# Column maxima of the slot logits: spread to all partitions by two DMAs through memory in place of TensorE products and VectorE copies

## The chip, the cores and the metric

The kernel runs on one core of a Trainium2 chip. The metric is the device time of one launch in microseconds (us), as the median of several executions; lower is better. Five engines work side by side and meet only at semaphores: TensorE (PE; PEld is its weight load), VectorE (DVE), ScalarE (ACT), GpSimd (POOL) and SyncE (SP), which issues all DMAs of this kernel.

## The reference, cut to what matters

A cross-attention block is followed by a soft mixture of experts. The change lies in the second part. With two batches of 1024 tokens, 16 experts of 64 slots (1024 slots in all) and width 256:

```python
logits   = einsum('bnd,esd->bnes', x, se)                 # tokens by slots
dispatch = softmax(logits, axis=1)                        # over the tokens: one maximum a slot
combine  = softmax(logits.reshape(b, n, -1), axis=-1)     # over the slots: one maximum a token
slots    = einsum('bnd,bnes->besd', x, dispatch)
# 16 experts: gelu(slots @ Wg + bg) * (slots @ Wu + bu), then @ Wd + bd
out      = einsum('bns,bso->bno', combine, eout)
```

The softmax over tokens needs, for each batch and slot, the maximum over all 1024 tokens. The tokens lie in the 128 partitions (rows) and in 8 tiles of 128, the slots along the free axis, so the maximum has to be taken across partitions, and its negative has to be present in every partition before it can be added to the logits.

## The kernel before, in words

The program is a list of events, one list for all engines (`prologue + attention + logits + slots + experts + combine`). Each engine walks through the list in its own `step` function and does its part of each event. TensorE takes the list as it stands; VectorE, ScalarE and GpSimd take it through `later(...)`, which sorts the events by their place in the list plus an offset from a table (`LATER_SLOTS_ACT`, `LATER_SLOTS_DVE`, `LATER_SLOTS_POOL`). The place is an index, so an event that is taken out of one place and put in at another can change which of two other events comes first on an engine.

The events around the change, with the lines of the profile:

- `("x2T", i)`: TensorE transposes the normalized tokens of tile i (L1534); ScalarE and VectorE write them as a high and a low half, GpSimd makes another low half (L757). Before it, `("N2", i)` normalizes tile i on VectorE (L1213) and then, in two operations, on GpSimd (L752, L753).
- `("L", i)`: the logits of token tile i, 12 TensorE products of 512 columns (L1552); ScalarE copies them into `lsb` (L922), VectorE takes them into the running maximum `colmax` (L1235), SP stores them to memory (L625). There are 16 tiles, 8 a batch. `("A", i)`: VectorE's maximum of each token (L1240).
- `("MX", b, c)`: for batch b and half c of the slots (512 of them), TensorE transposes `colmax` in four pieces (L1561), and VectorE reduces them to `nb`, 128 partitions by 4, the negated maxima, one slot a partition (L1248).
- `("MB", b, c)`: TensorE multiplies `nb`, broadcast along the free axis, with the identity, four products of 128 by 128 (L1570), which leaves the 512 values in every partition; VectorE copies them to `nb_b` (L1253). As `nb` has room for one batch, the reduction for batch 1 waits for the product of batch 0.
- `("E", n)`: n counts 16 blocks of 128 slots, 8 a batch. GpSimd adds `nb_b` to the logits of the block (L773), into one of three buffers `disp_f`; ScalarE takes the exponential (L932). It is the only reader of `nb_b`. Blocks 0 to 3 read half 0 of batch 0, 4 to 7 half 1, 8 to 11 and 12 to 15 those of batch 1.
- `("H", n)`: ScalarE copies the high half of block n (L943), VectorE makes the low half (L1260). `("D", n)`: 24 TensorE products (L1585) of dispatch weights and tokens; the first 16 need the high half alone, the last 8 the low half. VectorE divides by the sum (L1266, L1267). `("sT", n)`: the transpose of the result (L1593).

Events that leave a result in one of the three accumulator banks (`acc_no`) take the banks in turn, and TensorE waits for the bank's reader three events back. SP is a queue in order: 16 stores of logits tiles, then a wait for eight blocks of `E` (L627), the bias loads (L633) and the loads of the expert weights (L645).

The batches' events stand like this before: `MX(0,0)` after `L(8)`, `MB(0,0)` after `L(10)`, `MX(0,1)` after `L(11)`, `MB(0,1)` after `L(13)`; after `L(15)` come `H(0) D(0) MX(1,0) H(1) MX(1,1) MB(1,0)`, and `MB(1,1)` follows `D(1)`.

Of the kernel before, what the change touches and what calls it, by code (L numbers as in the profile page):

```python
# [5 lines left out]
P = 128  # L6
# [84 lines left out]
    ("HT", 14), ("EO", 13), ("CT", 0, 0), ("HT", 15), ("CT", 0, 1), ("EO", 14), ("EO", 15), ("COa", 0),  # L91
]
SLOTS_HEAD = [
    ("H", 0), ("D", 0), ("MX", 1, 0), ("H", 1), ("MX", 1, 1), ("MB", 1, 0),
]
LOGITS_AT = {3: [('B', 0)], 8: [('MX', 0, 0)], 10: [('MB', 0, 0)], 11: [('E', 0), ('MX', 0, 1)], 12: [('E', 1)], 13: [('MB', 0, 1)], 15: [('E', 2)]}
LATER_SLOTS_ACT = {
# [78 lines left out]
def program(nc, io):  # L176
# [94 lines left out]
    for ev in prologue + attention + logits + slots + experts + combine:  # L271
        if ev[0] == "Y" and ev[1] == GROUPS - 1:
            continue
        if ev[0] in ("bias", "cT", "K", "V", "VT", "xT", "Q", "PV", "Y", "seT", "x2T", "MX", "MB", "D", "sT", "HT", "EO", "CO"):
            acc_no[ev] = len(acc_no)
        if ev[0] == "T":
            t_no[ev] = len(t_no)
        if ev[0] == "S":
            s_no[ev] = len(s_no)
        if ev[0] == "V":  # L280
            v_no[ev] = len(v_no)
        if ev[0] in ("cT", "K", "VT", "xT", "Q", "PV", "seT", "x2T", "sT", "HT"):
            high_no[ev] = len(high_no)
# [9 lines left out]
    in_order(later(logits + slots, LATER_SLOTS_ACT), {("W", e, w): no for (e, w), no in piece_no.items()})  # L293
    in_order(later(logits + slots, LATER_SLOTS_DVE), acc_no)
    in_order(later(experts, LATER_EXPERTS_DVE) + combine, acc_no)

    top = ExitStack()
    top.enter_context(nc.allow_non_contiguous_dma(reason="three bias vectors, one value a partition"))

    def sb(stack, name, shape, dt=F32):  # L300
        return stack.enter_context(nc.sbuf_tensor(name, shape, dt))
# [92 lines left out]
    colmax = sb(lg, "colmax", [P, B, ES])  # L394
    nb_b = sb(lg, "nb_b", [P, B, ES])
    den = sb(lg, "den", [P, 2])
    nb = sb(lg, "nb", [P, ST])
    slot_f = sb(lg, "slot_f", [P, 2, D])
    b_row_at = -(-nc.sbuf_base // 32) * 32
    lg.close()  # L400
# [90 lines left out]
    last_full, last_used = sem("last_full"), sem("last_used")  # L491
    l_full, l_ready, amax_ready, colmax_ready = sem("l_full"), sem("l_ready"), sem("amax_ready"), sem("colmax_ready")
    d_shift, d_exp, d_high, d_low = (sem(s) for s in ("d_shift", "d_exp", "d_high", "d_low"))
    b_pick_ready, b_zeros = sem("b_pick_ready"), sem("b_zeros")
    w_high, gate_low, up_low, down_low, down_low_dve, b_high, b_low, eo_high = (sem(s) for s in (
        "w_high", "gate_low", "up_low", "down_low", "down_low_dve", "b_high", "b_low", "eo_high"))
# [72 lines left out]
    def _(sp):  # L569
# [49 lines left out]
        sp.dma_start(sb_b[:], slot_b.unsqueeze(0).to_broadcast([P, D])).then_inc(d_se, 16)  # L619
        sp.dma_start(sc_b[:], scale.unsqueeze(0).to_broadcast([P, 1])).then_inc(d_se, 16)  # L620
        l_t = logits_dram.rearrange("(t p) s -> p t s", p=P)
        for i in range(TILES):

            sp.wait_ge(l_ready, 2 * (i + 1))
            sp.dma_start(l_t[:, i], lsb[:, i]).then_inc(d_lst, 16)  # L625

        sp.wait_ge(d_shift, ST)  # L627
        sp.wait_ge(colmax_ready, TB)
# [35 lines left out]
    def _(pool):  # L664
# [15 lines left out]
        def step(ev):  # L680
# [48 lines left out]
            elif ev[0] == "Y" and ev[2] == 1:  # L729
                g = ev[1]  # L730

                pool.wait_ge(mv2_ready, 2 * g + 2)
                v = mv2[:, 2 * g:2 * g + 2, 1]
                link(pool.tensor_tensor(norm2[:, 0], v, eps[:], ALU.add))
                link(pool.tensor_tensor(norm2[:, 1], norm2[:, 0], mhalf[:, 0:2], ALU.pow))
                link(pool.tensor_tensor(norm2[:, 2], v, norm2[:, 1], ALU.mult))
                link(pool.tensor_tensor(norm2[:, 3], norm2[:, 2], norm2[:, 1], ALU.mult))
                link(pool.tensor_tensor(norm2[:, 4], norm2[:, 3], eps[:], ALU.add))
                link(pool.tensor_tensor(norm2[:, 5], norm2[:, 4], mhalf[:, 0:2], ALU.pow))
                pool.tensor_tensor(rstd2[:, 2 * g:2 * g + 2], norm2[:, 5], norm2[:, 1], ALU.mult)\  # L740
                    .then_inc(rstd2_ready, 1)
            elif ev == ("SA", ST // 2):
                pool.wait_ge(se_var, 1)
                link(pool.tensor_tensor(srs[:, 0], smv[:, :, 1], eps[:, 0:1].to_broadcast([P, ST]), ALU.add))
                pool.tensor_tensor(srs[:, 1], srs[:, 0], mhalf[:], ALU.pow).then_inc(se_rstd, 1)
            elif ev[0] == "N2":
                i = ev[1]

                pool.wait_ge(x2_centered, i + 1)
                if i == 0:  # L750
                    pool.wait_ge(d_gain, 32)
                link(pool.tensor_tensor(x2f[:, i % 3], x2f[:, i % 3], gain[:], ALU.mult))  # L752
                pool.tensor_tensor(x2f[:, i % 3], x2f[:, i % 3], shift[:], ALU.add).then_inc(x2_ready, 1)  # L753
            elif ev[0] == "x2T":
                i = ev[1]
                pool.wait_ge(x2_high, i + 1)
                pool.tensor_tensor(x2[1][:, i, 0:D], x2f[:, i % 3], x2[0][:, i, 0:D], ALU.subtract).then_inc(x2_low, 1)  # L757
            elif ev[0] == "E":
                n = ev[1]
                b, t = divmod(n, ST)  # L760

                wait_used(pool, ("MB", b, 2 * t // ST))
                if n < 3:

                    if n == 2:
                        wait_done(pool, ("MX", 0, 1))
                    wait_used(pool, ("seT", ST - 1))
                else:

                    pool.wait_ge(d_exp, n - 2)  # L770
                    if n == 3:
                        pool.wait_ge(d_low, 1)
                pool.tensor_tensor(disp_f[n % 3][:], lsb[:, b * TB:(b + 1) * TB, t * P:(t + 1) * P],  # L773
                                   nb_b[:, b, t * P:(t + 1) * P].unsqueeze(1).to_broadcast([P, TB, P]), ALU.add)\
                    .then_inc(d_shift, 1)
            elif ev[0] == "W" and ev[1:] not in FIRST_LOW_DVE:
                weight_low(ev[1], ev[2])
            elif ev == ("B", 0):

                pool.wait_ge(last_used, 2)  # L780
                pool.memset(b_row[:].bitcast(F32), 0.0).then_inc(b_zeros, 1)
# [235 lines left out]
    def _(dve):  # L1017
# [34 lines left out]
        def step(ev):  # L1052
# [188 lines left out]
            elif ev[0] == "MX":  # L1241
                _, b, c = ev

                wait_done(dve, ev)
                if b:

                    wait_done(dve, ("MB", 0, c))
                dve.tensor_reduce(nb[:, 4 * c:4 * c + 4], acc(no).rearrange("p (t n) -> p t n", t=4), AX, ALU.max,  # L1248
                                  negate=True).then_inc(acc_free, 1)
            elif ev[0] == "MB":  # L1250
                _, b, c = ev
                wait_done(dve, ev)
                dve.tensor_copy(nb_b[:, b, c * 512:(c + 1) * 512], acc(no)).then_inc(acc_free, 1)  # L1253
            elif ev[0] == "H":
                n = ev[1]
                dve.wait_ge(d_high, n + 1)
# [84 lines left out]
    def _(pe):  # L1341
# [31 lines left out]
        def step(ev):  # L1373
# [182 lines left out]
            elif ev[0] == "MX":  # L1556
# [4 lines left out]
                    ins = pe.transpose(dst[:, t * P:(t + 1) * P], colmax[:, b, (4 * c + t) * P:(4 * c + t + 1) * P],  # L1561
                                       ident[:])
                ins.then_inc(acc_full, 1)
            elif ev[0] == "MB":
                _, b, c = ev
                dst = bank(ev)

                wait_used(pe, ("MX", b, c))
                for t in range(4):
                    ins = pe.matmul(dst[:, t * P:(t + 1) * P], nb[:, 4 * c + t:4 * c + t + 1].to_broadcast([P, P]),  # L1570
                                    ident[:], start=True, stop=True)
                ins.then_inc(acc_full, 1)
            elif ev[0] == "D":
                n = ev[1]
                b = n // ST
# [116 lines left out]
```

## Time and profile before

| | us |
|---|---|
| median of 3 executions | 544.42 |
| lowest, highest | 544.23, 544.68 |
| the profiled execution | 544.24 |
| span in its profile (first to last instruction) | 542.5 |
| PE, DVE, ACT, POOL busy | 530.0, 434.1, 402.2, 303.3 |

The profiled execution is the lowest but for 0.01 us; 1.7 us of it lie outside the span. Engine times in the profile are counted from the start of the span. A row of a timeline gives start, length, engine, line, operation, the tiles written and read, and how many instructions were merged; in brackets, the idle time before it and what ended it. Two operations that follow each other on an engine overlap by nearly 0.1 us, so what an operation takes out of its engine's time is the distance of two starts.

### The profile page before, as it was taken

The numbers are of one execution on the slowest core, as the hardware profiler recorded it, in microseconds if no ns is written. First come the engines' busy times: TensorE is split into PE (matmuls) and PEld (weight loads), VectorE is DVE, ScalarE is ACT, GpSimd is POOL, SyncE is SP. The second block draws the span as 40 slices with busy tenths as digits, with TensorE's granted clock in tenths as the row PEclk, the third lists the DMA queues.
The fourth block names the chain that finished last, engine by engine and source line by source line (L and its number), as shares of the span: only waits on it lengthen the run. The fifth ranks groups of instructions, "written<-read, shape, count | busy, mean of one in ns | idle before, by whom it ended". The sixth has DMA issues, their size and how long they took to land.

```text
span 542.5 us, 11967 instructions
## 1 busy us (share of the span) xinstructions
PE 530.0 (98%) x3896; PEld 499.8 (92%) x3896; DVE 434.1 (80%) x1305; ACT 402.2 (74%) x1098; POOL 303.3 (56%) x327
## 2 busy tenths in 40 slices
PE   6999999999999999999998999999999999999997
PEld 4889999999999999999997888999978888899997
DVE  6777878787897979899677998798699888865453
ACT  5879969596896959779564555788979889766562
POOL 6674654544545455454365768787467999910000
DMA  8635000000030000000001333150288888525551
GB/s 257 181 86 179 3 1 2 2 2 1 3 98 2 2 2 1 2 0 4 0 1 80 155 156 156 78 201 1 79 264 283 270 306 288 182 79 170 181 167 67
DMA packets 34901, 54.11 MB, mean 100 GB/s; under 512 B 3997, under 2 KB 21497, under 8 KB 34713
## 3 DMA queue, kind: packets, MB, share of 16 engines
q1 hardware_dynamic: 34841, 53.36, 29.7%
q8 instruction: 32, 0.52, 0.4%
q14 instruction: 28, 0.23, 0.1%
HBM read 40.54 MB, written 10.49 MB: 94 GB/s over the span
## 4 chain that ended last, share of the span: by engine, by line
PE 90%; ACT 4%; DMA 2%; POOL 1%; DVE 1%; issue 1%; SPq 0%; ACTq 0%; DVEq 0%
PE ps L1461 9%; PE ps L1585 9%; PE ps L1357 9%; PE ps L1369 8%; PE ps L1610 8%; PE ps L1499 8%; PE ps L1439 7%; PE ps L1552 7%; PE ps L1476 5%; PE ps L1632 4%; PE ps L1501 4%; PE ps L1644 3%; DMA wvo_raw<-in_L_xattn_Wo_dram 2%; ACT expo L885 1%; PE ps L1615 1%; PE ps L1622 1%
## 5 line engine op out<-in xcount | busy, mean ns | idle before, releaser
L885 ACT ACTIVATE expo<-expo,nmin 128x154 f32<-128x154 f32 x256 | 106.2, 423 | 5.3 <-DVE nmin L1135 4.8
L1135 DVE CUSTOM_DVE_ANT_0 expo<-ps,maskb 128x154 f32<-128x154 f32 x256 | 69.1, 312 | 11.9 <-PE ps L1461 11.9
L723 POOL TENSOR_TENSOR prob_t<-expo,prec 128x104 f32<-128x104 f32 x64 | 23.1, 360 | 89.3 <-DVE prec L1146 89.1
L726 POOL TENSOR_TENSOR prob<-expo,prec 128x512 f32<-128x512 f32 x64 | 66.8, 1043 | 0.0
L1461 PE MATMUL ps<-kbd,qT_high 128*128 128x308 f32 x256 | 61.1, 323 | 0.0
L1155 DVE TENSOR_TENSOR pT_low<-ps,pT_high 128x512 fp32r<-128x512 f32 (+1 forms) x96 | 57.2, 596 | 4.1 <-ACT pT_high L899 3.9
L788 POOL TENSOR_TENSOR w_gu_low<-w_raw,w_gu_high 128x1024 fp32r<-128x1024 f32 x17 | 50.3, 2966 | 16.2 <-ACT w_gu_high L835 16.1
L899 ACT CAST pT_high<-ps 128x512 fp32r<-128x512 f32 (+1 forms) x96 | 49.1, 513 | 10.8 <-PE ps L1476 8.1
L803 ACT ACTIVATE oT_high<-ps,bqv_c 128x256 fp32r<-128x256 f32 x64 | 29.8, 466 | 34.8 <-PE ps L1501 34.7
L885 ACT ACTIVATION_READ_ACCUMULATOR expo<-expo,nmin 128x1 f32 x256 | 50.3, 196 | 0.0
L1461 PEld LDWEIGHTS ps<-kbd,qT_high 128*128 128x128 f32 x256 | 39.8, 190 | 0.2
L1461 PE MATMUL ps<-kbd,qT_low 128*128 128x308 f32 x128 | 39.0, 304 | 0.0
L1476 PE MATMUL ps<-ident,prob 128*128 128x128 f32 x256 | 38.5, 273 | 0.1
L1369 PE MATMUL ps<-wvo_high,oT_high 128*128 128x256 f32 x128 | 37.0, 289 | 0.0
L1501 PE MATMUL ps<-pT_high,vt 104*128 104x256 f32 x128 | 36.3, 284 | 0.0
L1369 PE MATMUL ps<-wvo_high,oT_low 128*128 128x256 f32 x128 | 36.2, 283 | 0.0
L1369 PE MATMUL ps<-wvo_low,oT_high 128*128 128x256 f32 x128 | 36.0, 281 | 0.0
L1357 PE MATMUL ps<-eo_high,comb 128*128 128x256 f32 x256 | 34.6, 287 | 0.4 <-issue 0.4
L1032 DVE SCALAR_TENSOR_TENSOR oT_low<-ps,bqv_c,oT_high 128x256 fp32r<-128x256 f32 x64 | 30.3, 474 | 5.3 <-ACT oT_high L803 4.5
L922 ACT COPY lsb<-ps 128x512 f32<-128x512 f32 x32 | 17.2, 589 | 22.3 <-PE ps L1552 22.3
L1006 ACT CAST comb<-ps 128x512 fp32r<-128x512 f32 x32 | 17.2, 590 | 21.3 <-PE ps L1644 21.3
L1032 DVE SCALAR_TENSOR_TENSOR qT_low<-ps,bqv_c,qT_high 128x256 fp32r<-128x256 f32 x64 | 29.9, 468 | 3.7 <-ACT qT_high L803 3.6
(241 smaller groups left out, 1762.7 us busy)
## 6 DMA issues: line engine op xcount, KB each, us to landing
logits_dram<-lsb SPq DMA_DIRECT2D x16, 512.0 KB, 2.6
w_raw<-in_L_ffn_Wg_dram SPq DMA_DIRECT2D x16, 512.0 KB, 4.0
w_raw<-in_L_ffn_Wu_dram SPq DMA_DIRECT2D x16, 512.0 KB, 4.5
w_raw<-in_L_ffn_Wd_dram SPq DMA_DIRECT2D x16, 512.0 KB, 4.5
lraw<-logits_dram SPq DMA_DIRECT2D x13, 512.0 KB, 3.8
out_dram<-gate SPq DMA_DIRECT2D x16, 128.0 KB, 2.2
kbd<-keys SPq DMA_DIRECT2D x12, 154.0 KB, 2.8
wvo_raw<-in_L_xattn_Wv_dram SPq DMA_DIRECT2D x2, 512.0 KB, 7.0
```

Of the source, the lines that this page charges most:

```text
L726: pool.tensor_tensor(prob[:, n % 2, :, heads, :], expo[:, n % 2, pp, :, :, 0:P], prec[:, n % 2, pp].unsqueeze(3).to_broadcast([P, 2, 2, P] ...
L788: pool.tensor_tensor(low, w_raw[:, i % RAW].rearrange("p (k n) -> p k n", k=KD if w == 0 else FT), high, ALU.subtract).then_inc(low_made(e ...
L885: ins = act.activation(row, row, ACT.Exp, scale=-1.0, bias=nmin[:, n % 2, pp, j, h:h + 1], accum_out=psums[:, n % 2, pp, j, h:h + 1])
L899: act.copy(pT[0][0:rows, n % 2, 2 * t:2 * t + tiles], ps[0:rows, NS + k % NT, 0:tiles * 2 * P].rearrange("p (t n) -> p t n", t=tiles))\
L1032: dve.scalar_tensor_tensor(out=dst, in0=src, scalar=bias, in1=high, op0=ALU.add, op1=ALU.subtract)\
L1135: ins = dve.tensor_tensor_reduce(out=expo[:, n % 2, pp, j, h, :], in0=ps[:, s % NS, h * SK:(h + 1) * SK], in1=maskb[:, (2 * (n // QUADS) + ...
L1155: dve.tensor_tensor(pT[1][0:rows, n % 2, 2 * t:2 * t + tiles], ps[0:rows, NS + k % NT, 0:tiles * 2 * P].rearrange("p (t n) -> p t n", t=ti ...
L1357: ins = pe.matmul(dst[:, 0:D], combT[s][:, i % 2, t], eo[m][:, i // TB, t], start=(first and r == 0 and t == parts[0]), stop=(last and r = ...
L1369: ins = pe.matmul(dst, oT[s][:, p, j * P:(j + 1) * P], wo[m][:, p], start=(first and p == 0 and r == 0), stop=(last and p == PAIRS - 1 and ...
L1461: ins = pe.matmul(dst, qT[s][:, n % 2, pp, j * P:(j + 1) * P], kbd[:, b, m, p, :], start=(r == 0), stop=(r == 2))
L1476: ins = pe.transpose(ps[:, NS + k % NT, (2 * h + j) * P:(2 * h + j + 1) * P], prob[:, n % 2, j, 2 * t + h, 0:P], ident[:])
L1501: ins = pe.matmul(dst[:, 0:2 * P], vt[:, b, s, q, pp * P:(pp + 1) * P], pT[m][0:T4, n % 2, 4], start=False, stop=(r == 2))
```

## The change

`MB` is no event of TensorE and VectorE any more. SP does it, in the place that `MB` has in the list: it waits until `nb` is written, stores the 128 by 4 values to a row of 512 floats in memory, waits for that store, and loads the row into all 128 partitions of `nb_b`. GpSimd's `E` waits for the load. `nb` gets room for both batches, so the reduction for batch 1 waits for nothing but its own transposes. `MB` takes no accumulator bank any more. In the list, each `MB` now stands right behind its `MX` (but `MB(1,1)`, which stays behind `D(1)`), and the logits stores keep their order around it on SP.

```diff
 SLOTS_HEAD = [
-    ("H", 0), ("D", 0), ("MX", 1, 0), ("H", 1), ("MX", 1, 1), ("MB", 1, 0),
+    ("H", 0), ("D", 0), ("MX", 1, 0), ("MB", 1, 0), ("H", 1), ("MX", 1, 1),
 ]
-LOGITS_AT = {3: [('B', 0)], 8: [('MX', 0, 0)], 10: [('MB', 0, 0)], 11: [('E', 0), ('MX', 0, 1)], 12: [('E', 1)], 13: [('MB', 0, 1)], 15: [('E', 2)]}
+LOGITS_AT = {3: [('B', 0)], 8: [('MX', 0, 0), ('MB', 0, 0)], 11: [('E', 0), ('MX', 0, 1), ('MB', 0, 1)], 12: [('E', 1)], 15: [('E', 2)]}
...
-        if ev[0] in (..., "x2T", "MX", "MB", "D", "sT", "HT", "EO", "CO"):
+        if ev[0] in (..., "x2T", "MX", "D", "sT", "HT", "EO", "CO"):
             acc_no[ev] = len(acc_no)
...
+    nb_order = [ev[1:] for ev in logits + slots if ev[0] == "MX"]
+    nb_dram = nc.dram_tensor("column_max", (B, ES), F32, kind="Internal").ap()
...
-    nb = sb(lg, "nb", [P, ST])
+    nb = sb(lg, "nb", [P, B, ST])
...
-        for i in range(TILES):
-
-            sp.wait_ge(l_ready, 2 * (i + 1))
-            sp.dma_start(l_t[:, i], lsb[:, i]).then_inc(d_lst, 16)
+        def spread_max(b, c):
+
+            k = nb_order.index((b, c)) + 1
+            row = nb_dram[b, c * 512:(c + 1) * 512]
+            wait_used(sp, ("MX", b, c))
+            sp.dma_start(row.rearrange("(t p) -> p t", p=P), nb[:, b, 4 * c:4 * c + 4]).then_inc(d_nb_row, 16)
+            sp.wait_ge(d_nb_row, 16 * k)
+            sp.dma_start(nb_b[:, b, c * 512:(c + 1) * 512], row.unsqueeze(0).to_broadcast([P, 512])).then_inc(d_nb[b][c], 16)
+
+        for ev in logits + slots:
+            if ev[0] == "L":
+                i = ev[1]
+                sp.wait_ge(l_ready, 2 * (i + 1))
+                sp.dma_start(l_t[:, i], lsb[:, i]).then_inc(d_lst, 16)
+            elif ev[0] == "MB":
+                spread_max(ev[1], ev[2])
...
-                wait_used(pool, ("MB", b, 2 * t // ST))
+                pool.wait_ge(d_nb[b][2 * t // ST], 16)
...
                 wait_done(dve, ev)
-                if b:
-
-                    wait_done(dve, ("MB", 0, c))
-                dve.tensor_reduce(nb[:, 4 * c:4 * c + 4], ...
+                dve.tensor_reduce(nb[:, b, 4 * c:4 * c + 4], ...
-            elif ev[0] == "MB":
-                _, b, c = ev
-                wait_done(dve, ev)
-                dve.tensor_copy(nb_b[:, b, c * 512:(c + 1) * 512], acc(no)).then_inc(acc_free, 1)
...
-            elif ev[0] == "MB":
-                _, b, c = ev
-                dst = bank(ev)
-
-                wait_used(pe, ("MX", b, c))
-                for t in range(4):
-                    ins = pe.matmul(dst[:, t * P:(t + 1) * P], nb[:, 4 * c + t:4 * c + t + 1].to_broadcast([P, P]),
-                                    ident[:], start=True, stop=True)
-                ins.then_inc(acc_full, 1)
```

With the places of `MB` in the list, two neighbours change on other engines: on VectorE `A(8)` comes before `N2(12)` (it came behind it), and on ScalarE the order `H(0) E(1) L(15) H(1) E(2) H(2)` becomes `H(0) L(15) E(1) E(2) H(1) H(2)`. On TensorE and GpSimd the order of the events that remain is the same.

## Rows read from the trace of the kernel before

**Rows 1.** Waits of PE, 288 to 395 us: total, times, longest.
```profile
PE ps L1534 <- POOL x2f L753: 1.1, 1, 1.1
...
PE ps L1570 <- DVE nb L1248: 0.6, 1, 0.6
```
**Rows 2.** Waits of PE, 395 us to the end.
```profile
PE ps L1357 <- issue: 0.4, 1, 0.4
```
**Rows 3.** Chain that ended last, 320 to 352 us: start, us, what.
```profile
333.85 0.89 PE ps L1570 x8
...
340.53 2.89 PE ps L1585 x24
343.42 0.45 PE ps L1561 x4
...
348.93 0.89 PE ps L1570 x8
```
**Rows 4.** Timeline of PE, 318 to 357 us.
```profile
324.25 0.38 PE L1534 MATMUL ps<-ident,x2f 128*128 128x128 f32 x2
...
334.58 0.38 PE L1534 MATMUL ps<-ident,x2f 128*128 128x128 f32 x2
...
340.37 1.12 PE L1585 MATMUL ps<-x_high,disp_high 128*128 128x258 f32 x8
...
345.77 1.21 PE L1585 MATMUL ps<-x_high,wkq_high 128*128 128x258 f32 x8
```
**Rows 5.** Timeline of VectorE, 318 to 357 us.
```profile
319.41 0.68 DVE L1248 TENSOR_REDUCE nb<-ps 128x4 f32<-128x512 f32 x1
...
320.66 1.21 DVE L1240 TENSOR_REDUCE neg_amax<-lsb 128x1 f32<-128x1024 f32 x1
321.79 1.27 DVE L1235 TENSOR_TENSOR colmax<-ps,colmax 128x512 f32<-128x512 f32 x2
...
325.96 0.67 DVE L1253 COPY nb_b<-ps 128x512 f32<-128x512 f32 x1
326.56 0.41 DVE L1030 TENSOR_TENSOR x2T_low<-ps,x2T_high 128x256 fp32r<-128x256 f32 x1
...
341.78 1.28 DVE L1235 TENSOR_TENSOR colmax<-ps,colmax 128x512 f32<-128x512 f32 x2
```
**Rows 6.** Timeline of GpSimd, 318 to 357 us.
```profile
321.63 0.74 POOL L753 TENSOR_TENSOR x2f<-x2f,shift 128x256 f32<-128x256 f32 x1
...
328.86 2.41 POOL L773 TENSOR_TENSOR disp_f<-lsb,nb_b 128x1024 f32<-128x1024 f32 x1
...
332.10 0.74 POOL L752 TENSOR_TENSOR x2f<-x2f,gain 128x256 f32<-128x256 f32 x1 [0.23 <-DVE x2f L1213]
332.92 0.74 POOL L753 TENSOR_TENSOR x2f<-x2f,shift 128x256 f32<-128x256 f32 x1
...
355.30 2.40 POOL L773 TENSOR_TENSOR colmax<-lsb,nb_b 128x1024 f32<-128x1024 f32 x1 [0.86 <-ACT ps L932]
```
**Rows 7.** Timeline of ScalarE, 318 to 357 us.
```profile
341.76 1.03 ACT L943 CAST wkq_high<-ps 128x1024 fp32r<-128x1024 f32 x1
343.16 1.03 ACT L932 ACTIVATE ps<-colmax 128x1024 f32<-128x1024 f32 x1 [0.36 <-DVE colmax L1235]
```
**Rows 8.** DMA issues: count, KB each, median us from issue to landing.
```profile
logits_dram<-lsb SPq DMA_DIRECT2D x16, 512.0 KB, 2.6
...
bo_b<-in_L_xattn_bo_dram SPq DMA_DIRECT2D x1, 128.0 KB, 7.3
...
b_raw<-in_L_ffn_bu_dram SPq DMA_DIRECT2D x1, 32.0 KB, 1.8
...
sc_b<-in_L_ffn_scale_dram SPq DMA_DIRECT2D x1, 0.5 KB, 5.1
```
**Rows 9.** The tile `keys`, SP's time for an issue: ns min/median/max.
```profile
L607 SPq DMA_DIRECT2D kbd<-keys x12: 590/610/1367, 17.9 to 31.0; - x12
```
**Rows 10.** Waits of SP over the span: total, times, longest.
```profile
SPq L633 <- POOL disp_f L773: 9.3, 1, 9.3
```

More of the change, by code:

```diff
@@ L273, in program @@
             continue
-        if ev[0] in ("bias", "cT", "K", "V", "VT", "xT", "Q", "PV", "Y", "seT", "x2T", "MX", "MB", "D", "sT", "HT", "EO", "CO"):
+        if ev[0] in ("bias", "cT", "K", "V", "VT", "xT", "Q", "PV", "Y", "seT", "x2T", "MX", "D", "sT", "HT", "EO", "CO"):
             acc_no[ev] = len(acc_no)
@@ L295, in program @@
     in_order(later(experts, LATER_EXPERTS_DVE) + combine, acc_no)
+    nb_order = [ev[1:] for ev in logits + slots if ev[0] == "MX"]
+    assert [ev[1:] for ev in logits + slots if ev[0] == "MB"] == nb_order
+    nb_dram = nc.dram_tensor("column_max", (B, ES), F32, kind="Internal").ap()
     top = ExitStack()
@@ L493, in program @@
     d_shift, d_exp, d_high, d_low = (sem(s) for s in ("d_shift", "d_exp", "d_high", "d_low"))
+    d_nb_row, d_nb = sem("d_nb_row"), [[sem(f"d_nb{b}{c}") for c in range(2)] for b in range(B)]
     b_pick_ready, b_zeros = sem("b_pick_ready"), sem("b_zeros")
@@ L1244, in step @@
                 wait_done(dve, ev)
-                if b:
-                    wait_done(dve, ("MB", 0, c))
-                dve.tensor_reduce(nb[:, 4 * c:4 * c + 4], acc(no).rearrange("p (t n) -> p t n", t=4), AX, ALU.max,
+                dve.tensor_reduce(nb[:, b, 4 * c:4 * c + 4], acc(no).rearrange("p (t n) -> p t n", t=4), AX, ALU.max,
                                   negate=True).then_inc(acc_free, 1)
-            elif ev[0] == "MB":
-                _, b, c = ev
-                wait_done(dve, ev)
-                dve.tensor_copy(nb_b[:, b, c * 512:(c + 1) * 512], acc(no)).then_inc(acc_free, 1)
             elif ev[0] == "H":
```

## The prediction

> **What bounds the kernel now.** I read the views in this order: the waits of TensorE, the chain that ended last around the change, the timelines of the four engines there, and the DMA issues. The waits of TensorE say that it sets the pace: from 288 to 395 us, where logits and dispatch lie, it waits 1.1 us at the start (a normalization on GpSimd), 0.6 in front of one `MB` for `nb` [rows 1], and else only at the very end of the stage; from 395 us on it waits 0.4 us in all [rows 2]. None of the `D` products waits for its operands. So a microsecond that leaves TensorE's queue here is won at the end, if no other engine takes up the slack. The chain runs through the `MB` products, 0.89 us each [rows 3]. The timelines must then tell how far behind TensorE the others are, and there the margin is thin.
>
> **What is removed, and what then holds TensorE.** Four `MB` of four products leave TensorE, at 0.89 us each [rows 3], and four copies leave VectorE, each taking 326.56 - 325.96 = 0.60 us of it [rows 5]. I go along the list.
>
> (1) `MB(0,0)`. Without it TensorE would come to the transpose `x2T(12)` at 324.25 - 0.89 = 323.36 us [rows 4]. But on VectorE `A(8)` now stands ahead of `N2(12)`. `A(8)` takes 321.79 - 320.66 = 1.13 us [rows 5], so `N2(12)` is that much later, and GpSimd's second half of it ends at 321.63 + 0.74 + 1.13 = 323.50 [rows 6]; with some 0.14 us for the semaphore TensorE starts at 323.64. That gives 324.25 - 323.64 = 0.61, not 0.89.
>
> (2) `MB(0,1)`. TensorE's next transpose, `x2T(15)`, started at 334.58 [rows 4] and could come 0.61 + 0.89 = 1.50 earlier, at 333.08. It needs `N2(15)`, for which GpSimd had waited 0.23 us on VectorE [rows 6]; VectorE is ahead by its one copy so far, 0.60. GpSimd's end moves from 332.92 + 0.74 = 333.66 to 333.06, and with 0.14 the transpose starts at 333.20. Gain so far: 334.58 - 333.20 = 1.38. The last two logits tiles follow without a gap, and `D(0)` starts 1.38 earlier.
>
> (3) From `D(0)` to `D(1)`. Before, 345.77 - 340.37 = 5.40 us [rows 4]. Two `MX` of 0.45 behind the 2.89 of `D(0)` [rows 3] would leave 3.79. But ScalarE now does `E(2)` ahead of `H(1)`. `E(2)` needs the maximum of tile 15: VectorE's two operations for it end at 341.78 + 1.28 = 343.06, 2.69 behind the start of `D(0)`, and nothing in front of them is faster now (the low half of block 0, which waits for the end of `L(15)`). So `E(2)` starts 2.79 behind `D(0)`, as before, at 343.16 against 340.37 [rows 4, 7]; `H(1)`, which used to run ahead of it at 341.76, starts some 0.95 later, takes 1.03 [rows 7], and with 0.12 for the semaphore `D(1)` starts 2.79 + 0.95 + 1.03 + 0.12 = 4.89 behind `D(0)`. Gain 5.40 - 4.89 = 0.51; without the new order it would be 1.6. What is late next is the low half of block 1; at the 1.21 us of VectorE's other operation on 128 by 1024 [rows 5] it is done before `D(1)` asks for it, 16 of its 24 products or 1.9 us later.
>
> (4) `MB(1,1)` between `D(1)` and `sT(0)`: 0.89 [rows 3]. VectorE is two copies lighter there, so the other blocks keep their margin. `H(1)` lies later against TensorE than before, and `E(3)` with it, but 16 products of `D(1)` and all of `D(2)` lie ahead of the use.
>
> Sum: 1.38 + 0.51 + 0.89 = 2.78 us. Two smaller edits cost nothing: `nb` for two batches takes a wait away that had long been met, and with fewer takers of banks the tightest is `D(1)` on the bank of `D(0)`, whose two short readers on VectorE run while TensorE does the `MX` and waits for `H(1)`.
>
> **What is added.** Four pairs of DMAs, in series, on SP. The trace before shows neither, so I bound a pair from both sides. The store has 512 pieces of 4 bytes. SP took 0.61 us to issue 256 pieces (64 partitions by 4 runs) [rows 9], so 1.2 us for 512; the smallest loads landed 1.8 us after issue [rows 8], which holds about 0.4 of issue. That gives 1.8 + 0.8 = 2.6 us. The load has 128 pieces of 2 KB, 256 KB: between 1.8 us for 32 KB and 2.6 for 512 KB [rows 8], I take 2.4. A pair is then about 5.2 us with its two semaphores. The lower bound is 3.6 (twice 1.8). The upper is 12.4: the one load of 4-byte pieces landed after 5.1 us and the first row spread to all partitions after 7.3 [rows 8], both behind other transfers. I take 5.2, nearer the low end, because SP's queue holds only one logits store a tile here, which lands in 2.6.
>
> The Trainium skill, "DMA: Bandwidth & Descriptors", section "Rules for kernel authors", speaks against the store: a last dimension that is not contiguous becomes a descriptor for each element, and should be rearranged. By its section "Anatomy of one DMA", with about 2.0 us fixed for each transfer (given for another issuing path) and the bytes at 436 GB/s, a pair would be an estimated 4.6 us, and the sum above would stay as it is. The 1.8 us of the smallest loads agrees with the first figure; no row shows the price of 512 elements.
>
> What hides the pairs: `nb(0,0)` is written at 319.41 + 0.68 = 320.09 [rows 5], and `E(0)` began at 328.86, straight behind other work of GpSimd [rows 6]; it would begin at 328.26. A pair may take 8.2 us, 8.4 with the 0.2 us that GpSimd waits later. The other three have more: `MX(0,1)` lies a stage earlier than its first reader `E(4)`, and `nb(1,0)`, reduced behind transposes that end at 343.42 + 0.45 = 343.87 before [rows 3], is read by `E(8)` at 355.30 [rows 6], 11 us behind; both come earlier after. Behind SP's waits stand logits stores, which nobody awaits until the bias loads, and there SP had idled 9.3 us for GpSimd [rows 10]; two pairs end within that, as the second one's store need not wait for the first one's load. If the cover is gone, `E(0)` holds up `N2(15)` behind it on GpSimd, that `x2T(15)`, and each microsecond beyond 8.4 is one lost.
>
> The profiled execution took 544.24: 544.24 - 2.78 = 541.46. The median of the runs is 0.18 higher, so I forecast 541.6.
>
> **Rivals.** *The full price of the products.* If neither `N2(12)` nor `H(1)` comes late, all four `MB` and the wait in front of the third are won: 0.89 + 0.89 + (5.40 - 3.79) + 0.89 = 4.28, 540.1 on the median's scale. For it: the waits show only what happened before. Against: both orders are in the code, and the rows give them lengths. Chance 0.08.
>
> *The gain goes back in the dispatch stage.* If some `D(n)` now waits for its low half, what is won from `D(1)` on (0.51 + 0.89) is lost and 1.38 stays: 543.0. For it: VectorE and ScalarE are busy there as well, and `H(1)` starts behind TensorE's clock by a microsecond more. Against: no `D` waited in 50 us [rows 1] and VectorE has two copies less. Chance 0.10.
>
> *The first pair is slow.* The place is `E(0)` on GpSimd. At 8.4 us nothing is lost, at 8.4 + 2.78 = 11.2 us all is given back, and at the upper bound of 12.4 the kernel takes 541.6 + 4.0 = 545.6, slower. For it: 512 pieces of 4 bytes, and the 7.3 and 5.1 us of the nearest forms. Against: those stood in a queue of large loads. Chance 0.10, with about half of it beyond 11.2.
>
> **How the numbers follow.** The forecast, 541.6 give or take 0.5, has 0.72. The range for 8 in 10 runs from 540.4 to 543.1; it leaves out the full price below and most of the slow pair above. A difference of 0.2%, 1.1 us, is about what a measurement of this kernel can tell from no change. Faster by more than that: the forecast, the full price, most of the second rival and a little of the third, 0.87. The same: 0.07. Slower: a pair beyond 12.3 us or something that I don't see, 0.06.
>
> **What would show it.** In the profile after, no L1570 and no L1253 row; `x2T(12)` waits 0.3 us on GpSimd and `x2T(15)` 0.1; `D(1)` starts 4.9 us behind `D(0)`, with about 1.1 us of waiting for ScalarE's `H(1)`; no `E` waits for a DMA; the `D` stage keeps its period; the experts run as before, 2.8 us earlier. It is wrong if GpSimd's first `E` waits for `nb_b`, if `D(2)` to `D(15)` show waits, or if `H(1)` runs in time.

## The result, and the profile after

The kernel after takes 556.18 us (median of 4 executions, 554.66 to 557.87), the kernel before beside it 544.55 (544.23 to 545.21): ratio 1.0214, 95% interval 1.0193 to 1.0236. The prediction was 541.6, in a range from 540.4 to 543.1. The change makes the kernel slower by 11.6 us.

The profiled execution took 557.58 us, 13.34 more than the profiled one of before, and its span is 555.6; TensorE's mean granted clock was 0.988. The four executions lie at 554.7, 554.8, 557.6 and 557.9 us, with mean granted clocks of 0.991, 0.993, 0.988 and 0.988, so the profiled one is of the slower two, and what follows accounts for its 13.3 us, not for the 11.6 of the medians.

Waits of TensorE from 288 to 420 us, beside [rows 1]; total, times, longest:

```profile
PE ps L1545 <- POOL x2f L771: 6.2, 2, 5.1
PE ps L1587 <- ACT disp_high L961: 5.4, 1, 5.4
```

L1545 are the `x2T` transposes, L1587 the `D` products. Of the 6.2, 1.1 is the wait at the start of the stage that [rows 1] has too. Two waits of over 5 us are new. The chain that ended last names what released them (start, us, what):

```profile
320.09 8.98 DMA column_max<-nb
...
329.08 4.72 DMA nb_b<-column_max
...
338.43 0.66 PE ps L1545 x2
...
374.74 4.83 DMA b_raw<-in_L_ffn_bd_dram
...
379.59 0.03 ACT b_row L979
...
382.21 5.50 PE ps L1587 x24
```

The first pair of DMAs and the last bias load have entered the chain, where the prediction had all of them hidden. The first pair takes from 320.09 to 333.8, 13.7 us, where 5.2 were predicted and 8.4 were covered: 8.98 for a store of 2 KB, then 4.72 for the load. On GpSimd, `E(0)` and `E(8)` wait over 5 us for a load (and `E(12)` 3.37); beside [rows 6]:

```profile
333.86 2.34 POOL L791 TENSOR_TENSOR disp_f<-lsb,nb_b 128x1024 f32<-128x1024 f32 x1 [5.57 <-DMA nb_b<-column_max]
...
366.06 2.40 POOL L791 TENSOR_TENSOR colmax<-lsb,nb_b 128x1024 f32<-128x1024 f32 x1 [5.77 <-DMA nb_b<-column_max]
```

The other three pairs are no faster. SP's timeline (L633 store, L635 load, L651 bias loads; logits stores are left out; the length is that of the issue alone):

```profile
320.09 0.37 SPq L633 DMA_DIRECT2D column_max<-nb  x1
329.08 0.32 SPq L635 DMA_DIRECT2D nb_b<-column_max  x1
...
331.23 0.98 SPq L633 DMA_DIRECT2D column_max<-nb  x1
344.50 0.32 SPq L635 DMA_DIRECT2D nb_b<-column_max  x1
...
351.13 0.37 SPq L633 DMA_DIRECT2D column_max<-nb  x1
361.22 0.32 SPq L635 DMA_DIRECT2D nb_b<-column_max  x1
361.58 0.43 SPq L633 DMA_DIRECT2D column_max<-nb  x1
373.39 0.32 SPq L635 DMA_DIRECT2D nb_b<-column_max  x1
373.90 0.34 SPq L651 DMA_DIRECT2D b_raw<-in_L_ffn_bg_dram  x1
```

Each load's issue follows the landing of its store: 9.0, 13.3, 10.1 and 11.8 us behind the store's. SP is an ordered queue, so each late store pushes what stands behind it: logits stores, the next pair, and at the end the bias loads, which go out at 373.90. The waits of SP answer to [rows 10]: the 9.3 us in which SP waited for GpSimd in front of the bias loads are gone, and it waits 41.9 for its own stores:

```profile
SPq L635 <- DMA column_max<-nb: 41.9, 4, 12.3
```

The data of the first store are through long before it counts as landed. Stretches of the trace: length, each engine's busy time (instructions), granted clock, busy share of the 16 DMA engines, GB/s:

```profile
321.00:322.00 1.00, 1.00 (x7) 0.83 (x6) 1.00 (x3) 1.00 (x3) 0.09 (x1) 1.00 0.25 2
322.00:324.00 2.00, 2.00 (x12) 1.60 (x11) 2.00 (x5) 0.65 (x4) 1.92 (x3) 1.00 0.00 0
...
355.00:361.00 6.00, 6.00 (x53) 6.00 (x51) 5.96 (x11) 4.38 (x8) 5.23 (x3) 1.00 0.00 0
367.00:373.00 6.00, 6.00 (x53) 6.00 (x52) 4.33 (x11) 3.87 (x7) 6.00 (x3) 1.00 0.00 0
```

From 322 us the DMA engines move nothing, and the store counts as landed at 329.08: seven microseconds in which the trace shows nothing but its completion outstanding. The same stands behind each of the four stores: the DMA engines are idle from about 322.0, 337.3, 354.1 and 366.0 us, and the stores count as landed 7.1 to 7.4 us later. In what comes before that, 1.9 to 6.1 us, the four differ, and there, besides the store's own data, logits stores or the load of the pair before are moving.

The Trainium skill, "DMA: Bandwidth & Descriptors", section "Anatomy of one DMA", says that a transfer's semaphore fires only when its last byte is confirmed in the target memory, and that HBM is the heaviest target for this; it puts the whole fixed cost at about 2 us (for another issuing path). The order of events agrees with this trace, the size does not.

The rest of the loss is TensorE's clock. The same view, around the two gaps of TensorE:

```profile
333.00:337.00 4.00, 0.36 (x2) 0.00 (x0) 0.00 (x0) 0.76 (x1) 3.14 (x3) 1.00 1.00 392
337.37:344.19 6.82, 5.76 (x16) 4.63 (x17) 3.17 (x5) 2.22 (x7) 6.74 (x6) 0.53 0.00 0
...
381.74:388.57 6.83, 6.36 (x31) 6.39 (x32) 5.55 (x10) 5.96 (x12) 4.53 (x2) 0.53 0.62 206
389.00:407.00 18.00, 17.88 (x150) 17.64 (x148) 12.17 (x30) 16.64 (x29) 8.51 (x4) 1.00 0.21 61
```

In each of the two gaps of TensorE, which had been busy up to them, the granted clock fell from 2.4 GHz to its lower level, 1.2 GHz (0.53 of full speed in each of the two stretches shown), and it stayed there for some 6.8 us, into the work behind the gap. Timeline of TensorE, with the idle time in brackets, beside [rows 4]:

```profile
338.43 0.66 PE L1545 MATMUL ps<-ident,x2f 128*128 128x128 f32 x2 [5.07 <-POOL x2f L771]
346.70 1.13 PE L1587 MATMUL ps<-x_high,disp_high 128*128 128x258 f32 x8
...
351.61 1.22 PE L1587 MATMUL ps<-x_high,wkq_high 128*128 128x258 f32 x8 [0.95 <-ACT wkq_high L961]
...
382.21 2.06 PE L1587 MATMUL ps<-x_high,disp_high 128*128 128x258 f32 x8 [5.41 <-ACT disp_high L961]
```

With the same starts in the trace of before, the distances on TensorE give the account, us:

| stretch | before | after | difference |
|---|---|---|---|
| start to `x2T(11)` | 320.32 | 320.75 | +0.43 |
| `x2T(11)` to `x2T(15)` | 14.26 | 17.68 | +3.42 (5.07 of waiting, less 1.8 for two `MB`) |
| `x2T(15)` to `D(0)`, two logits tiles | 5.79 | 8.27 | +2.48 (lower clock) |
| `D(0)` to `D(2)` | 9.42 | 8.03 | -1.39 (the gain of `MB(1,0)`, `MB(1,1)`) |
| `D(2)` to `D(8)` | 18.74 | 18.72 | 0 |
| `D(8)` to `D(9)` | 3.10 | 8.76 | +5.66 (bias loads, below) |
| `D(9)` to `D(11)` | 6.22 | 8.86 | +2.64 (lower clock) |
| `D(11)` to `D(15)` | 12.42 | 12.43 | 0 |

The sum is 13.2 of the 13.34. `D(9)` waits for the high half of its block, `H(9)` on ScalarE; in front of `H(9)` stands the conversion of the expert biases to `b_row` (L979), and that waits 7.36 us for the last bias load, which SP could issue only behind the fourth pair:

```profile
379.59 1.26 ACT L979 CAST b_row<-b_raw 16x1280 fp32r<-16x1280 f32 x1 [7.36 <-DMA b_raw<-in_L_ffn_bd_dram]
```

### The profile page after: what moved, and what is told of

Its sections match the earlier page's. It is cut to its first block, busy times and chain, and to the rows that moved or that the text cites. A ratio compares the mean times of both kernels' runs of the same rounds, so it can differ in the third digit from the quotient of the medians.

```text
span 555.6 us, 11901 instructions
## 1 busy us (share of the span) xinstructions
PE 532.0 (96%) x3864; PEld 500.2 (90%) x3864; DVE 432.0 (78%) x1301; ACT 402.4 (72%) x1098; POOL 303.3 (55%) x327
## 2 busy tenths in 40 slices
DMA packets 37589, 55.17 MB, mean 99 GB/s; under 512 B 6173, under 2 KB 23673, under 8 KB 37401
## 4 chain that ended last, share of the span: by engine, by line
PE 80%; DMA 6%; DVE 5%; ACT 4%; issue 2%; POOL 2%; SPq 0%; DVEq 0%; ACTq 0%
PE ps L1472 8%; PE ps L1368 8%; PE ps L1380 8%; PE ps L1612 8%; PE ps L1587 8%; PE ps L1510 8%; PE ps L1450 7%; PE ps L1487 4%; PE ps L1634 4%; PE ps L1512 4%; PE ps L1646 3%; PE ps L1563 2%; DMA wvo_raw<-in_L_xattn_Wo_dram 2%; DMA column_max<-nb 2%; ACT expo L903 1%
## 5 line engine op out<-in xcount | busy, mean ns | idle before, releaser
L791 POOL TENSOR_TENSOR disp_f<-lsb,nb_b 128x1024 f32<-128x1024 f32 x11 | 26.2, 2387 | 15.9 <-DMA nb_b<-column_max 8.9
L1061 DVE TENSOR_TENSOR w_gu_low<-w_raw,w_gu_high 128x1024 fp32r<-128x1024 f32 x14 | 30.4, 2171 | 3.6 <-ACT w_gu_high L853 3.6
```

## The experiments

Every kernel below starts from the kernel after. Their own ratios are to runs of the kernel before on the same chip.

### Without the pairs

```diff
-            elif ev[0] == "MB":
-                spread_max(ev[1], ev[2])
+                if i == 3:                    # behind logits store 3
+                    for b, c in ...:
+                        sp.dma_start(nb_b[...], const_dram[b]...to_broadcast([P, 512]))
```

> This kernel leaves the column maxima out: nb_b gets a constant a batch (-220 and -56), loaded from memory at the fourth logits tile, and no store or load of maxima is issued; all else is as in the changed kernel, with the new orders on VectorE and ScalarE. Theory 1 (all of the loss comes from the pairs of DMAs being late, and the sum of the prediction is right without them): 541.6 us, 2.8 below the kernel before, no wait of GpSimd for a DMA, D(1) about 4.9 us behind D(0). Theory 2 (the new orders, or the bank count, cost time by themselves): at or above 544. Theory 3 (the products were worth their full price): 540.1.

Measured: 542.54 us (541.72 to 543.48), ratio 0.9961, 0.9946 to 0.9976; profiled execution 541.72. Of TensorE's waits in the logits and dispatch stages the longest, beside the one at the start, is the predicted one in front of `D(1)`:

```profile
PE ps L1598 <- ACT wkq_high L970: 1.0, 1, 1.0
```

The time is 2.2 us below that of the kernel before by the medians (1.3 to 2.9 by the interval) and 2.5 by the profiled executions, where the prediction had 2.78. So what the edits on TensorE, VectorE and ScalarE do together agrees with the prediction within the noise, and the loss lies in the pairs.

### What the delay reaches: the biases, `E(0)`, and both

`bias_ahead` issues the bias loads between the last store and its load:

```diff
             sp.dma_start(row.rearrange("(t p) -> p t", p=P), nb[...]).then_inc(d_nb_row, 16)
+            if (b, c) == (1, 1):
+                load_biases()
             sp.wait_ge(d_nb_row, 16 * k)
```

> The changed kernel, but SP issues the three bias loads between the store and the load of the last pair, so that they wait for no pair but the third. Theory 1 (the loss has two places, E(0) behind the first pair and the bias copy on ScalarE behind SP's waits; each brings a stretch of TensorE at the lower clock): the 5.4 us wait of D(9) for H(9) and its slow stretch of some 3 us go, the wait of 5.1 us in front of x2T(15) stays; about 548, 547 to 550. Theory 2 (D(9) is held by the late load of the last pair through E(12), not by the biases): 554 or more, and the wait of D(9) stays.

`e0_later` gives GpSimd's `E(0)` a place behind `N2(15)` and the low half of `x2T(14)`, so that it holds up no transpose, and leaves the bias loads where they were:

```diff
 LATER_SLOTS_ACT = {
-    "GU": 3.5, ("E", 0): 6, ...
+    "GU": 3.5, ("E", 0): 12, ...
 LATER_SLOTS_POOL = {
-    ... ("MX", 1, 1): -0.5, ("E", 0): -0.5, ...
+    ... ("MX", 1, 1): -0.5, ("E", 0): 8, ("E", 1): 3, ...
```

> The changed kernel, but E(0) stands behind N2(15) and the low half of x2T(14) on GpSimd, E(1) behind the low half of x2T(15), and E(0) behind L(14) on ScalarE. Theory 1: the 5.1 us wait in front of x2T(15) and the slow clock after it (some 2.5 us) go, the wait of D(9) stays: about 549, 548 to 551. Theory 2 (the pairs slow TensorE by their traffic, or the logits stores held back on SP are what is missed): no gain, 555 or more.

`both` has the two edits together.

> The edits of bias_ahead and e0_later together; the stores and loads of the maxima are as slow as in the changed kernel. Theory 1: both losses go and the gain of the removed products is left, 542 to 543.5. If part of the loss has a third place (a late E(4) or E(12), traffic): above 545.

Measured: `bias_ahead` 550.83 us (549.38 to 554.57), ratio 1.0123, 1.0085 to 1.0161. `e0_later` 555.97 (554.67 to 557.22), 1.0215, 1.0192 to 1.0238: no gain at all. `both` 551.06 (549.53 to 551.77), 1.0113, 1.0093 to 1.0133: no better than `bias_ahead` alone. In `bias_ahead` the wait of `D(9)` is gone and the one in front of `x2T(15)` stays, as its theory 1 said; the median lies 0.8 above that theory's range:

```profile
PE ps L1550 <- POOL x2f L776: 4.6, 1, 4.6
```

The slow stretch behind this gap is shorter than in the kernel after: the granted clock is 0.50 from 338 to 340 us and 1.00 again from 342, and the two logits tiles up to `D(0)` take 7.27 us, not 8.27. So what a gap costs on top of itself was not one figure.

The waits of TensorE in `e0_later`, from 310 to 420 us:

```profile
PE ps L1587 <- DVE sT_low L1285: 4.8, 1, 4.8
PE ps L1587 <- ACT disp_high L961: 2.7, 1, 2.7
```

The 5.07 us in front of `x2T(15)` is gone, as intended, and `D(0)` starts at 338.80. But SP has not become faster. Its timeline in `e0_later`, third and fourth pair:

```profile
347.02 0.55 SPq L633 DMA_DIRECT2D column_max<-nb  x1
362.47 0.32 SPq L635 DMA_DIRECT2D nb_b<-column_max  x1
362.83 0.43 SPq L633 DMA_DIRECT2D column_max<-nb  x1
372.12 0.32 SPq L635 DMA_DIRECT2D nb_b<-column_max  x1
372.63 0.34 SPq L651 DMA_DIRECT2D b_raw<-in_L_ffn_bg_dram  x1
```

The third store, issued 4.1 us earlier than in the kernel after, lands 1.2 us later. What `E(0)` no longer costs is waited for at `D(8)`, since `E(8)` needs the third load, and at `D(9)`, since the biases go out at 372.63. The releaser that the row names in front of `D(8)`, `sT_low`, is the end of that chain: ScalarE waits 6.34 us for `E(8)`, and only behind `E(8)`, `H(8)` and `E(9)` does it copy the `sT` whose accumulator bank `D(8)` takes. So `e0_later` has the time of its theory 2, but by neither of the causes that the theory gave. In `both` the biases are out of the way. GpSimd waits there for the second and the fourth load too (4.2 us at `E(4)`, 2.3 at `E(12)`), but only its wait for the third, at `E(8)`, reaches TensorE. Waits of GpSimd and of TensorE in `both`:

```profile
POOL colmax L796 <- DMA nb_b<-column_max: 7.1, 1, 7.1
POOL disp_f L796 <- DMA nb_b<-column_max: 6.5, 2, 4.2
...
PE ps L1592 <- DVE sT_low L1290: 4.5, 1, 4.5
```

There are thus three places at which the series of stores holds TensorE, `E(0)`, `E(8)` and the biases, one behind the other. My account of the kernel after had two, since there TensorE, late already by `E(0)`, has no wait at `D(8)`. Mending the places, with the stores as slow as they are, brought the kernel to 550.8 us at best, still above the kernel before.

### Why the store is slow: shape against number

`store_16B` writes the same bytes to the row in another order: 128 pieces of 16 bytes, each partition's four values side by side.

```diff
-            sp.dma_start(row.rearrange("(t p) -> p t", p=P), nb[...])
+            sp.dma_start(row.rearrange("(p t) -> p t", t=4), nb[...])
```

The row then holds the slots in another order.

> The changed kernel with one edit: the store writes the 4 values of a partition side by side, so it has 128 pieces of 16 bytes and not 512 of 4. The row in memory is then in another order than the slots, so each slot gets the maximum of another slot of its half as its shift. Theory 1 (the time of the store goes with its pieces: about 7.3 of its 9 us lie behind the moment when its data have passed the DMA engines, and 512 pieces are four times 128): the first store lands after 3.5 to 4.2 us; the first pair takes 8.5 us and E(0) waits at most 1; the biases are in time; the kernel takes 542 to 543.5. Theory 2 (a store to memory takes 9 us here whatever its pieces, because of the logits stores around it): 9 us again, 554 to 558.

`store_apart` keeps the 512 pieces of 4 bytes, but writes them 512 bytes apart. The loads bring a constant row.

```diff
-    nb_dram = nc.dram_tensor("column_max", (B, ES), F32, kind="Internal").ap()
+    nb_dram = nc.dram_tensor("column_max", (B, ES, P), F32, kind="Internal").ap()
-            row = nb_dram[b, c * 512:(c + 1) * 512]
+            row = nb_dram[b, c * 512:(c + 1) * 512, 0]
```

> The store keeps its 512 pieces of 4 bytes but writes them 512 bytes apart from each other in memory; the load takes a row of constants (-220 and -56 by batch, written at 150 us) in place of the maxima, still behind the store. This leaves the maxima out. Theory 1 (the price goes by the piece): the store lands after 9 us alone, 9 to 15 behind logits stores, as in the changed kernel, 555 to 558 in all. Theory 2 (the price comes from pieces of different partitions that fall into the same stretch of memory): 2.5 to 4 us, 542 to 544. For the load: 4.7 us again if that is what a row for all partitions costs; 2.4 to 3 if it was slow because the row had just been written.

`spacing` looks for the distance at which the effect ends:

```diff
+            n = (4, 8, 16, 32)[2 * b + c]       # 16, 32, 64, 128 bytes
+            row = nb_dram[2 * b + c, 0:512 * n].rearrange("(s n) -> s n", n=n)[:, 0]
```

> Where 4-byte pieces stop to disturb each other. The four stores write 512 pieces of 4 bytes each, 16, 32, 64 and 128 bytes apart in this order; the loads bring a constant row, so the maxima are left out. Theory 1 (a store is slow while pieces of several partitions fall into one short stretch of memory, and the stretch is 64 bytes or so): the store at 16 bytes 5 to 9 us, at 32 bytes 3 to 6, at 64 and 128 bytes 1.8 to 2.5 as with 512 bytes. Theory 2 (the stretch is 512 bytes): all four are slow, 128 bytes 3 us or more. Theory 3 (it is enough that the pieces are not next to each other): all four land in 1.8 to 2.5. Time 542 to 548, by whether the first, second and third store land late.

Measured: `store_16B` 541.94 us (540.89 to 543.81, 10 executions), ratio 0.9959, 0.9945 to 0.9972. `store_apart` 542.42, one execution. `spacing` 544.74, one execution, so of these two the rows count and not the times; what it has more than `store_apart` it has ahead of the first pair (`x2T(11)` at 322.82 against 320.11). SP's timeline in `store_apart`, first pair, and in `spacing`, the stores at 16, 32 and 128 bytes with the issue of the load behind them:

```profile
319.88 0.37 SPq L639 DMA_DIRECT2D column_max<-nb  x1
321.71 0.32 SPq L642 DMA_DIRECT2D nb_b<-constant_row  x1
```

```profile
322.16 0.37 SPq L640 DMA_DIRECT2D column_max<-nb  x1
324.59 0.32 SPq L643 DMA_DIRECT2D nb_b<-constant_row  x1
...
331.69 0.37 SPq L640 DMA_DIRECT2D column_max<-nb  x1
333.66 0.32 SPq L643 DMA_DIRECT2D nb_b<-constant_row  x1
...
348.25 0.42 SPq L640 DMA_DIRECT2D column_max<-nb  x1
351.55 0.32 SPq L643 DMA_DIRECT2D nb_b<-constant_row  x1
```

512 pieces of 4 bytes land 1.8 us after issue when they are 512 bytes apart, and 2.4, 2.0, 2.0 and 3.3 at 16, 32, 64 and 128 bytes; the last goes out right behind a load of 256 KB, as that of `store_apart`, which takes 3.1. Side by side they take 9.0 to 13.3 (15.4 in `e0_later`). So it is not the number of pieces, which the count of DMA packets under 512 bytes confirms: 6173 in the kernel after and 6461 in `store_apart`, which has two rows of constants more, against 4637 where the four stores have 128 pieces each (`strided`, below). It is that pieces of 4 bytes, which come from neighbouring partitions, lie side by side. Theory 3 of `spacing` holds, but for the store behind the load, and the other two fall. 16 bytes written as one piece next to 16 bytes of the next partition are fast too: 2.2 and 1.9 us for the first two stores of `store_16B`, less than the 3.5 to 4.2 that its theory 1 worked out from a quarter of the pieces. Neither a distance of 8 bytes nor separate pieces of one partition side by side were tried, and what it is in the memory that delays the completion stays open.

For the load, `store_apart` gives 3.2 us in the median for a row of constants written long before, and the versions that read a row just written give 3.6 to 3.7. So having just been written is worth at most half a microsecond of the 4.7 in the kernel after; there three logits stores go out right behind the first load, and no run separates what they add.

The Trainium skill, "DMA: Bandwidth & Descriptors", section "Rules for kernel authors", advises against a last dimension that is not contiguous, as it becomes a descriptor for each element. The advice is right here, but for another reason than the one it gives: `store_apart` has a descriptor for each element as well, and is fast.

### The row made by TensorE

```diff
+    pe.transpose(dst[0:4, 0:P], nb[:, b, 4 * c:4 * c + 4], ident[:])     # event MB, behind MX
+    dve.tensor_copy(nb_t[:, b, c], acc(no)[0:4, 0:P])
-    sp.dma_start(row.rearrange("(t p) -> p t", p=P), nb[...])
+    sp.dma_start(row.rearrange("(t p) -> t p", p=P), nb_t[:, b, c])      # 4 pieces of 512 bytes
```

> TensorE transposes the 128 by 4 maxima (one product of 128 columns) and VectorE copies the 4 by 128 result, so that the store has 4 pieces of 512 bytes; the load is as in the changed kernel. MB stands behind L(9) for the first half, behind L(13) and D(1) for the others, and ScalarE keeps the order of the kernel before (H(1) ahead of E(2)). Theory 1 (few pieces make a fast store): the store lands after 2 to 2.5 us and the pair takes 7 us; E(0) waits 0 to 1.5 us; of the 4.3 us that the four products were worth, four transposes of 0.11 and the wait of E(0) are lost: 541 to 542. Theory 2 (a store of maxima is slow whatever its pieces): 9 us again, above 550.

Measured: 543.75 us (542.77 to 547.07, 9 executions), ratio 0.9993, 0.9977 to 1.001: no difference from the kernel before, where theory 1 had 541 to 542. The first pair is the fastest of all, 1.17 us from the store's issue to the load's, and no block waits for a DMA. But the events on TensorE and the copies on VectorE are back, and so is a wait of 0.9 us for that copy in front of `D(2)`:

```profile
PE ps L1601 <- DVE nb_t L1273: 0.9, 1, 0.9
```

With this wait and one of 0.6 in front of `sT(0)`, the way from `D(1)` to `D(2)` takes 5.25 us in the profiled execution, against 4.02 before.

### Two versions that beat both kernels

`strided` has the 16-byte pieces and the row in the order of the slots. The transposes in front take every fourth column of `colmax`, so that four neighbouring slots lie in one partition:

```diff
+                cols = colmax[:, b, c * 512:(c + 1) * 512].rearrange("p (n t) -> p t n", t=4)
                 for t in range(4):
-                    ins = pe.transpose(dst[:, t * P:(t + 1) * P], colmax[:, b, (4 * c + t) * P:(4 * c + t + 1) * P], ident[:])
+                    ins = pe.transpose(dst[:, t * P:(t + 1) * P], cols[:, t], ident[:])
...
-            sp.dma_start(row.rearrange("(t p) -> p t", p=P), nb[...])
+            sp.dma_start(row.rearrange("(p t) -> p t", t=4), nb[...])
```

> The transposes before the store take every fourth column of the running maximum, so that a partition holds four neighbouring slots and the store writes 128 pieces of 16 bytes, with the row in the order of the slots. Theory 1 (only the shape of the store cost the time; the permuted row of the run with 16-byte pieces had no part in its speed): 541.9 us, 541.3 to 542.6, ratio 0.9955; store 2.0 us, load 3.6, no block of the dispatch waits for a DMA, TensorE waits only 1.0 in front of D(1). Theory 2 (a column stride of 16 bytes slows TensorE's transposes): each of the four MX longer than 0.60 us in TensorE's rows; at twice the length of a transpose, 16 times 0.14 = 2.2 us, three quarters of it on the path: about 543.5.

`strided_order` also puts ScalarE's `H(1)` ahead of `E(2)` again, by one offset of `LATER_SLOTS_ACT`, `("E", 2): 5` to `6`.

> As the strided version, and ScalarE does H(1) ahead of E(2) again (one offset, 5 to 6). Theory 1 (the 1.0 us in front of D(1) is the order alone and nothing else is late behind it): D(1) starts 3.8 behind D(0) in place of 4.9, 1.1 us less than the strided version, 540.8 us (540.2 to 541.4), ratio 0.9935. Theory 2 (what D(1) gains is lost again at D(1)'s low half, at D(2) or at sT(0), since E(2) and its H come later): a wait of up to 1 us moves there, 541.5 to 542.5, no difference from the strided version.

Measured: `strided` 541.87 us (541.47 to 542.67), ratio 0.9954, 0.994 to 0.9967. `strided_order` 541.04 (540.34 to 542.04), ratio 0.9937, 0.9924 to 0.995. Theory 1 holds in both. TensorE's `D(0)` and `D(1)`, first in `strided`, then in `strided_order`:

```profile
338.98 1.13 PE L1587 MATMUL ps<-x_high,disp_high 128*128 128x258 f32 x8
...
343.88 1.20 PE L1587 MATMUL ps<-x_high,wkq_high 128*128 128x258 f32 x8 [0.86 <-ACT wkq_high L961]
```

```profile
340.46 1.12 PE L1587 MATMUL ps<-x_high,disp_high 128*128 128x258 f32 x8
...
344.31 1.23 PE L1587 MATMUL ps<-x_high,wkq_high 128*128 128x258 f32 x8
```

4.90 us become 3.85, and no wait takes the place of the one that went. The medians differ by 0.8; the two intervals overlap, so between these two versions the rows are the evidence, not the times. Both intervals against the kernel before lie below 1 by more than 0.3%.

## Why the prediction was wrong

**The sum of the gains was right, within what the executions differ.** Where the pairs are hidden, the terms can be read off one by one, in `strided`:

- Steps 1 and 2: from `x2T(11)` to `D(0)`, 20.05 us before by the table (14.26 + 5.79) and 338.98 - 320.27 = 18.71 there: 1.34, predicted 1.38. The split was off there. `x2T(12)` came 0.93 earlier, the full price of `MB(0,0)`, and not 0.61: `A(8)` ahead of `N2(12)` cost TensorE nothing. `x2T(15)` came 1.77 earlier, and the last logits tiles gave back 0.43, 0.2 of it a wait for VectorE's running maximum, where I had them follow without a gap. In part the rival of the full price, in part one that I had not listed. But it goes by execution: in the traces of `strided_order`, `store_apart` and `store_16B` `x2T(12)` came 0.62 to 0.65 earlier, as forecast, and steps 1 and 2 together gave 1.02 to 1.05. The two starts in `strided`:

```profile
320.27 0.38 PE L1545 MATMUL ps<-ident,x2f 128*128 128x128 f32 x2
...
323.27 0.38 PE L1545 MATMUL ps<-ident,x2f 128*128 128x128 f32 x2
```

- Step 3: `D(0)` to `D(1)` predicted 4.89, measured 4.90 there and 4.91 in the kernel after, with the wait for `H(1)` (0.9 us; 1.1 predicted). `strided_order` shows that the new order of ScalarE is its cause, and that it is worth 1.05 (1.1 predicted).
- Step 4: `D(1)` to `D(2)` 4.02 before, 3.11 there: 0.91, predicted 0.89.
- The dispatch stage gave nothing back: `D(2)` to `D(8)` keeps its 18.7 us.

In the profiled executions `strided` is 2.64 us faster than before, against a sum of 2.78.

**The step that failed is the cost of the pair.** The sign of being wrong that the prediction named is in the trace: GpSimd's first `E` waits 5.57 us for `nb_b`. I put the store at 2.6 us, as 1.2 of issue for 512 pieces and a landing like that of the smallest loads. The issue took 0.37. The store landed 9.0 us after issue, 7.1 of them behind its last data: I had priced the pieces by their number [rows 9] and not by where they fall, and the 256 pieces of the row that I scaled from do not show that. The load took 4.7 in place of 2.4 (3.6 in the median of each of the two versions above). The pair of 13.7 us lies above my upper bound of 12.4, which I had made of the one load of 4-byte pieces and the one row spread to all partitions [rows 8]: no row of before showed a store of neighbouring pieces, so the bound stood on loads. And I took a value near the low end for the reason that SP's queue was nearly empty; but the delay comes with no transfer in the queue.

**The rival was the right mechanism, at a fraction of its price.** The slow first pair was there, with its place at `E(0)` and its break-even at 11.2 us, and by its rule 13.7 us would have cost 13.7 - 8.4 - 2.78 = 2.5 us, 547 in all. Two things were missing. First, that SP's queue is a series: I had looked for cover behind the first pair and let two pairs end within SP's 9.3 idle us [rows 10]. The four stores kept SP waiting 41.9 us, and `E(8)` and the bias loads behind it became bounds (`bias_ahead`, 5.4 us faster by the medians; `both`). Second, TensorE's clock: the two gaps drew two stretches at the lower clock behind them, 2.5 and 2.6 us by the table above. Neither appears in [rows 1], where TensorE never idles so long.

## What to carry to other kernels

A DMA that is to be hidden is to be priced by the layout of its destination, down to the distance between neighbouring pieces, and by its landing, not by its bytes or its count of pieces; where no row shows that layout, the cover must be held against a bound from much further off. Where the layout is bad, the cheap remedy is to change what lies in a partition one step earlier, here by a stride in the operand of a transpose that is done anyway. And where several such DMAs stand in series on one queue, follow the queue to its last entry: the harm was done at least as much by what came behind them as by the first reader.

## What the runs showed of the hardware

- A store of 512 pieces of 4 bytes that lie side by side, neighbours from neighbouring partitions, lands 9.0 to 15.4 us after issue; in the kernel after, the DMA engines are idle for the last 7.1 to 7.4 us of that in each of the four. The same pieces 16 bytes apart land in 2.4, 512 bytes apart in 1.8, and 128 pieces of 16 bytes side by side in about 2; the fourth stores, behind a load, take 3.1 to 3.6.
- Issuing 512 pieces took SP 0.37 to 0.43 us in three of the four stores and 0.98 in the other, less than the 0.61 for the 256 pieces of `keys` [rows 9] but for that one.
- In gaps of TensorE of 5.1 and 5.4 us the granted clock fell, and was 0.53 of full speed over 6.8 us, which is the level of 1.2 GHz but for the edges; in `e0_later`, the gaps that moved to `D(8)` and `D(9)` cost clock as well (0.90 from 345 to 380 us). Behind the gap of 4.6 us in `bias_ahead` the slow stretch was shorter (1.00 again from 342 us, where the work had begun at 337.5).
- Transposes of columns 16 bytes apart took little longer than those of neighbouring columns: four in 0.63 us in `strided`, 0.60 in the kernel after.
